# Pre-norm attention and three-matrix FFN on 8 cores: reordered head with one power per tile, 34 identity matmuls ahead of it, and a new count of folds per head pair

## The reference

```python
def _L0_attn_ref(x, Wq, Wk, Wv, Wp):          # x: (8, 2048, 1024)
    q = (x @ Wq).reshape(B, N, H, K)          # 16 heads of 64
    k = (x @ Wk).reshape(B, N, H, K)
    v = (x @ Wv).reshape(B, N, H, V)
    scores = jnp.einsum('bnhk,bmhk->bhnm', q, k) * scale
    attn = jax.nn.softmax(scores, axis=-1)
    out = jnp.einsum('bhnm,bmhv->bnhv', attn, v).reshape(B, N, D)
    return x + out @ Wp
...
def _L0_ffn_ref(x, weight, aux_weight1, aux_weight2, bias):
    h = x @ weight; h = h @ aux_weight1; h = h @ aux_weight2
    return jnp.tanh(h + bias)
...
x = x + _L0_attn_ref(_layernorm(x), Wq, Wk, Wv, Wp)
x = x + _L0_ffn_ref(_layernorm(x), weight, aux_weight1, aux_weight2, bias)
```

## Time and profile before

| | |
|---|---|
| median of 3 runs | 729.91 us (729.4 to 729.97) |
| the profiled execution's own time | 729.96 us |
| its span, slowest core (core 6) | 728.2 us |
| spans of the 8 cores | 725.1 to 728.2 us |
| mean granted clock of each core | 0.998 to 1.000 |
| PE busy / ACT busy / DVE busy / POOL busy | 681.6 / 599.4 / 264.4 / 125.3 us |
| head, to the first exponential (core 6) | 61.5 us |
| main loop, 8 head pairs | 61.5 to 622.6 us |
| tail | the rest, 105.6 us |

### The profile page before, as it was taken

The page is one execution under the profiler, slowest core; times in us unless marked ns, Lnnn a source line. Parts: engine busy times, 40 slices in busy tenths (PEclk is TensorE's granted clock), DMA queues, the critical chain, the costliest instruction groups (busy, mean ns, idle before and its releaser), DMA issues.

```text
span 728.2 us, 21958 instructions; the slowest of 8 cores (725.1 to 728.2 us)
## 1 busy us (share of the span) xinstructions
PE 681.6 (94%) x9112; PEld 432.3 (59%) x9112; DVE 264.4 (36%) x590; ACT 599.4 (82%) x600; POOL 125.3 (17%) x169
## 2 busy tenths in 40 slices
PE   1699999999999999999999999999999989999996
PEld 0465676667666765676667656665676555444443
DVE  4724322332223322322332233224322343556663
ACT  2566999999999999999999989999999899444443
POOL 5871000000000002000000000012010121366654
PEclk9999999999999999999999999999999999999999
DMA  8959700111010004610110000032024000334332
GB/s 229 283 72 166 135 9 3 16 16 16 4 16 2 2 3 69 107 17 2 17 22 12 16 2 3 2 88 88 2 41 80 1 3 2 109 124 155 134 116 116
DMA packets 13344, 41.87 MB, mean 57 GB/s; under 512 B 1600, under 2 KB 1728, under 8 KB 13248
## 3 DMA queue, kind: packets, MB, share of 16 engines
q0 software_dynamic: 5904, 15.21, 13.7%
q1 hardware_dynamic: 7056, 25.17, 10.4%
q10 hardware_dynamic: 288, 0.10, 0.1%
HBM read 46.76 MB, written 8.39 MB: 76 GB/s over the span
## 4 chain that ended last, share of the span: by engine, by line
PE 86%; DVE 4%; issue 3%; DMA 3%; ACT 3%; POOL 0%; DVEq 0%; SPq 0%; ACTq 0%; POOLq 0%
PE sc L370 18%; PE pv L398 16%; PE fl L217 14%; PE fl L256 8%; PE sc L521 5%; PE fl L343 4%; PE fl L326 4%; PE sc L464 4%; PE fl L464 3%; ACT P L382 2%; DMA aoT<-x 2%; PE fl L422 2%; PE sc L217 1%; DMA wv<-wqkv 1%; PE pv L521 1%
## 5 line engine op out<-in xcount | busy, mean ns | idle before, releaser
L382 ACT ACTIVATE P<-sc,cb 128x1024 bf16<-128x1024 f32 x512 | 528.3, 1114 | 36.4 <-PE sc L370 24.4
L398 PEld LDWEIGHTS pv<-v,P 128*128 128x128 bf16 x4096 | 157.7, 97 | 44.1 <-issue 17.2
L398 PE MATMUL pv<-v,P 128*128 128x65 bf16 x4096 | 173.5, 193 | 5.4 <-DVE ao L414 2.6
L370 PE MATMUL sc<-qT,kT 64*128 64x256 bf16 x2048 | 157.5, 272 | 1.8 <-ACT P L382 1.8
L370 PEld LDWEIGHTS sc<-qT,kT 64*128 64x128 bf16 x2048 | 78.5, 94 | 42.8 <-issue 25.2
L532 ACT ACTIVATE S<-S 128x512 f32<-128x512 f32 x32 | 20.1, 629 | 58.2 <-DVE S L528 58.2
L256 PE MATMUL fl<-wv,S 128*128 128x128 bf16 x960 | 63.6, 219 | 1.8 <-DVE aoT L429 0.4
L256 PEld LDWEIGHTS fl<-wv,S 128*128 128x128 bf16 x960 | 54.1, 98 | 12.4 <-issue 12.2
L217 PE MATMUL fl<-S,wq 128*128 128x512 bf16 x224 | 57.8, 380 | 0.5
L217 PE MATMUL fl<-S,wk 128*128 128x512 bf16 x208 | 53.5, 380 | 3.1 <-DVE ao L414 1.3
L268 DVE CAST v<-fl 128x512 bf16<-128x512 f32 x29 | 20.0, 691 | 78.8 <-PE fl L256 78.8
(11 more groups left out here) (128 smaller groups left out, 555.8 us busy)
## 6 DMA issues: line engine op xcount, KB each, us to landing
xs<-x SPq DMA_DIRECT2D x22, 512.0 KB, 6.0
out<-S SPq DMA_DIRECT2D x15, 512.0 KB, 2.9
aoT<-x SPq DMA_DIRECT2D x8, 512.0 KB, 12.7
wk<-wqkv POOLq DMA_DIRECT2D x8, 256.0 KB, 9.0
wq<-wqkv POOLq DMA_DIRECT2D x8, 256.0 KB, 4.9
wv<-wqkv POOLq DMA_DIRECT2D x8, 256.0 KB, 5.9
bufA<-w1t POOLq DMA_DIRECT2D x4, 512.0 KB, 14.3
bufB<-w POOLq DMA_DIRECT2D x4, 512.0 KB, 25.0
```

What stands on the lines that cost most here:

```text
L370: ins = TE.matmul(sc[s][:, 512 * h + QC * i:512 * h + QC * (i + 1)], kT[p % 2][64 * h:64 * (h + 1), 128 * m:128 * (m + 1)], qT[p % 2][64 * ...
L382: exp_in[t] = s_se.inc(SE.activation(P[t % NPB][:], sc[s][:], AF.Exp, bias=cb[p % 2][:], scale=0.125))
L398: ins = TE.matmul(bank[PV0][:, col:col + 65], P[t % NPB][:, off:off + 128], v[p % 2][:, VW * (2 * m + h):VW * (2 * m + h) + 65], start=(u ...
```

## The change

There are three parts.

1. **The head.** `ln1_tile` takes each tile on its own: DVE also writes minus the mean (`ngm`); POOL makes one power for the tile, and only for every fourth tile the product `nm`; the other tiles are normalised as (x + ngm) * rs, tile 15 on DVE. The first slice, `wk` of pair 0, is issued once tile 0 has landed and no longer at the start; `wk` of pair 1 is issued in group 0 of the loop. K and Q of a group now stand ahead of the transposes of the next tiles on PE, V ahead of the two after them, and K of pair 1 for the same group at the end, for groups 0, 1 and 2. The squares of groups 0 to 2 move ahead of the last K and Q. V of group 3 is cut into 12, 8 and 12 matmuls around the guards. `nm` for all tiles is made by one more DVE instruction behind the squares.
2. **34 matmuls** of the identity with itself on PE, ahead of the first transpose, once `identb` and `identf` have landed.
3. **The folds.** Pair 0 has one K unit of pair 1 less to run, since three are in the head; `N_FOLD` becomes 8, 4, 4, 4, 4, 4, 4 where it was 7, 4, 4, 4, 4, 5, 4. The lines that treat pair 3 by themselves stay.

```diff
-        w_in = {(1, 0): load_slice(1, 0)}
+        w_in = {}
...
+        def ln1_tile(t):
             need(VE, x_in[t])
...
+            m = s_ve.inc(VE.bn_aggr(mv[:, 2 * t:2 * t + 2], st[:]))
             need(VE, m)
-            m = s_ve.inc(VE.tensor_scalar(ve[:, t:t + n], var, EPS, None, ALU.add))
+            s_ve.inc(VE.tensor_scalar(ngm[:, t:t + 1], mv[:, 2 * t:2 * t + 1], -1.0, None, ALU.mult))
+            m = s_ve.inc(VE.tensor_scalar(ve[:, t:t + 1], mv[:, 2 * t + 1:2 * t + 2], EPS, None, ALU.add))
             need(GP, m, gp_ones)
+            m = s_gp.inc(GP.tensor_tensor(rs[:, t:t + 1], ve[:, t:t + 1], mhalf[:, 0:1], ALU.pow))
+            if t % 4 == 0:
+                need(GP, m)
+                nm_in[t] = s_gp.inc(GP.tensor_tensor(nm[:, t:t + 1], ngm[:, t:t + 1], rs[:, t:t + 1], ALU.mult))
+                return
+            eng, sem = (VE, s_ve) if t == NT - 1 else (GP, s_gp)
+            need(eng, m, t1_mm.get(t - 2 * NXN))
+            xn_in[t] = sem.inc(eng.tensor_scalar(xn1[t % (2 * NXN)][:], x_tile[t], ngm[:, t:t + 1],
+                                                 rs[:, t:t + 1], ALU.add, ALU.mult))
...
+        need(TE, const_in)
+        for _ in range(34):
+            TE.matmul(bank[7][:, 0:128], identb[:], identb[:], start=True, stop=True)
+        need(GP, x_in[0])
+        w_in[(1, 0)] = load_slice(1, 0)
+        for t in range(4):
+            ln1_tile(t)
+            if t == 0:
+                ln1_se(0)
+            if t == 1:
                 w_in[(0, 0)] = load_slice(0, 0)
+            ln1_turn(t, SE, s_se)
+        w_in[(2, 0)] = load_slice(2, 0)
+        for g in range(NT // 4 - 1):
+            t0 = 4 * g + 4
+            for t in range(t0, t0 + 2):
+                ln1_tile(t)
+            ln1_se(t0)
+            if g == 0:
                 w_in[(1, 1)] = load_slice(1, 1)
+            bk = first_proj(1, 0, g)
+            bq = first_proj(0, 0, g)
+            evict_qk(1, 0, g, bk, SE, s_se)
+            for t in range(t0, t0 + 2):
+                ln1_turn(t, SE, s_se)
+                if t == t0:
+                    evict_qk(0, 0, g, bq, SE, s_se)
+            for t in range(t0 + 2, t0 + 4):
+                ln1_tile(t)
+            bv = first_proj(2, 0, g)
+            if t0 + 4 == NT:
+                for h in range(3):
+                    square(1, 0, h)
+                    square(0, 0, h)
+            ln1_turn(t0 + 2, SE, s_se)
+            evict_v(0, g, bv, SE, s_se)
+            ln1_turn(t0 + 3, *((VE, s_ve) if t0 + 4 == NT else (SE, s_se)))
+            bk = first_proj(1, 1, g)
+            evict_qk(1, 1, g, bk, SE, s_se)
...
-        N_FOLD = [7, 4, 4, 4, 4, 5, 4]
+        N_FOLD = [8, 4, 4, 4, 4, 4, 4]
...
-            for g in range(2 if p == 0 else 0, 4):
+            for g in range(3 if p == 0 else 0, 4):
                 units.append(unit_k(p + 1, g))
```

More of the change, by code:

```diff
@@ L657, in build_program @@
         ring["i"] = 0
[L658 removed]
+        b = next_bank()
+        values = v_mms(0, 3, b)
+        for _ in range(12):
+            next(values)
         guard1(0, next_bank())()
```

72 lines of the change are left out of this document (10 added, 62 removed).

## The result

| | before, same chip | after |
|---|---|---|
| median | 729.94 us (729.4 to 730.28, 4 runs) | 738.71 us (737.96 to 740.56, 4 runs) |
| ratio after / before | | 1.0125, 95% interval 1.0105 to 1.0144 |
| profiled execution, slowest core | 729.96 us, core 6, span 728.2 | 740.56 us, core 4, span 738.9 |
| mean span of the 8 cores | 726.8 us | 735.1 us |

What follows compares the result with a forecast made beforehand. The prediction took PE to bound the kernel, with ACT waiting for it in the loop. From 729.96 us, -2.5 (head) - 2.7 (pair 5) + 12.0 (stall) + 1.7 (clock) - 1.3 (excess) = +7.2 gave 737.2 us, range 733.0 to 740.5.

Steps and rivals of the forecast that it cites:

- part 1, pair 5: Pair 5 of the main loop: 16 fillers instead of 17 make it 2.7 us shorter, bounds -1.7 and -3.2.
- part 2, pair 3 in all: Pair 3: the wait for w3 (+12.0), a clock restart (+1.7) and the pair's own excess dropping out (-1.3).
- part 3, head: Start to first exponential: reordered tiles, slices and PE work bring it 2.5 us sooner, bounds 0 and -4.5.
- part 4, 34 matmuls: Head, ahead of the first transpose: identity matmuls fit in idle PE time, cost 0 and gain 0.
- pair 0: First pair of the loop: one K unit less and one fold more, 16 units as before, change 0.
- tail: After the last pair: said not to be touched, so no term in the sum.
- The stall: Pair 3's first unit_w123: PE waits for late pieces of w3 and loses 12.0 us, bounds +8.4 and +13.
- The restart of the clock: Behind the wait in pair 3: one spell of PE at the lower clock, +1.7 us, bounds 0 and 3.4.
- Pair 3's own excess: Pair 3's extra 1.4 us, seen only with the w3 transfer, mostly vanishes while PE stands still: -1.3.
- (a): Pair 3: shorter stall of +8.4 as on core 0, clock stays up, 731.9 us; chance 0.18.
- (b): Head: gains nothing, as slices back to back hold K of pair 1 until 35; 739.7 us, chance 0.13.
- (c): Pair 3: the wait for w3 costs nothing and both gains remain, 724.8 us; chance 0.05.

Runs made afterwards that it cites:

- e3_folds_only: The kernel before, head untouched, with N_FOLD 7, 5, 4, 4, 4, 4, 4, so pair 1 has the 17th unit; 740.9 us, ratio 1.0158.
- e6_wk1_early: e1_plain_order with the wk slice of pair 1 issued right behind wv, ahead of tiles 4 and 5; 724.86 us, ratio 0.9935.
- e1_plain_order: The changed kernel without the two lines that pull pair 3's first fold ahead of the K units; 725.84 us, ratio 0.9959.
- e2_fold_two_units_later: The changed kernel with pair 3's first fold placed behind two K units; 729.37 us, ratio 1.0001.
- e7_head_only: The changed kernel with the old fold numbers 7, 4, 4, 4, 4, 5, 4; 729.56 us, ratio 1.0007.

## Why the prediction was right

It gave 737.2 us, 733.0 to 740.5; 738.7 was measured, and the mechanism was the one named. That the sum came within 1.5 us owes something to luck: two terms that were put at nothing cost 1.7, and pair 3 cost 0.8 less than forecast. (The ends of the range lie 0.5 and 0.8 us outside the sums that their reasons give, 733.5 for a stall of 10 without restart and 739.7 for no gain in the head.) Step by step:

| step | predicted | measured, mean of 8 cores |
|---|---|---|
| part 1, pair 5 | -2.7 | -2.6 |
| part 2, pair 3 in all (12.0 + 1.7 - 1.3) | +12.4 | +11.6; +12.2 on core 6 |
| part 3, head | -2.5 | -2.6; -1.8 over several kernels |
| part 4, 34 matmuls | 0 | 0 in the head |
| pair 0 | 0 | +0.8 |
| tail | 0 | +0.9 |
| pairs 1, 2, 4, 6, 7 | 0 | +0.2 |
| sum | +7.2 | +8.4; medians +8.8 |

**Pair 5** was right: 71.88 to 69.32, and `e3_folds_only` shows the same 2.4 to 2.7 for a 17th unit in another pair.

**The stall** was right in its place, its cause and its form: on core 4 four waits ended by `bufA`, pieces of 1.5 to 3.1 us (9.8 in sum where 11 to 12 were expected; slow matmuls between them fill the rest), and landings of the fourth piece 12.8 to 17.1 us after its issue, against the 14.0 to 17.6 of the earlier trace rows. The step that carried it was to count the landings from the first issue and to set them against the place of the reader. On core 4 the last two matmuls would have stood at 277.5 (8.8 us behind the row at 268.69, as in the earlier trace rows from 269.88 to 278.7) and stood at 289.04: 11.5 against the 12.0 forecast. The fit of the Trainium skill, *DMA: Bandwidth & Descriptors*, section "Anatomy of one DMA", would have had all four pieces there 6.8 us after the first issue; on core 4 it took 1.6 + 17.1 = 18.7, and no core was under 1.6 + 12.8 = 14.4. That estimate counts the bf16 bytes; w3 is float32 in memory, and with those 4.2 MB the same fit gives an estimate of 11.6, still less than any core took. The measurement decides against the page for four such converting loads queued together.

**The restart of the clock** was right in kind and too small: 1.7 forecast, 2.2 measured. It was taken from 8 matmuls of K in the head that ran slow. Here all of PE's work from 289.04 to 294.89 ran slow: two fold matmuls, P times V, Q times K, five of K and P times V again. The slow matmuls before that cost nothing, since the next piece was still under way. As for the 1.00 that the windows of the head read beside a slow K: the trace's clock record begins only at 27.36 there (core 6), where that K ends (23.64 + 3.57 = 27.21), and 1.00 is what the window shows where there is no record.

**Pair 3's own excess**, -1.3, was a misreading. It was read from the slowest core alone (70.58); on seven cores pair 3 was 69.2 to 69.6 before. One core's difference between two of its pairs was taken for an effect of the transfer. For core 6 itself it fits (82.77 - 70.58 = 12.2, against 12.4), for the others not. This error and the small restart both made the forecast of pair 3 too small. What made up for them is the stall itself: by the landings (landing of the fourth piece less 7.3 us) it is 7.1 to 11.3 us by core, mean 9.6, against the 12.0 forecast. As a mean 9.6 + 2.2 - 0.1 gives the 11.6 within 0.1; on core 6, 11.3 + 2.2 - 1.3 is its 12.2.

**The head** came out right as a sum in this execution, with 1.8 rather than 2.6 over several kernels, and two of its steps were off. The statistics of tile 3 began 2.2 us sooner (means of 12.19 and 14.42; 2.5 on core 6), not 1.2, so K of group 0 began at 19.75 on core 6, the core that the forecast was worked out on, not 20.3, and V at 26.21, not 27.1. V waited for `wv` on four cores only. But as worked out, K of pair 1 then waits for its slice: 31.10 against 31.2. That wait swallowed the surplus, and on cores 4 and 5 the clock fell around it, which was not foreseen; `e6_wk1_early` frees another 1.2 us by issuing the slice sooner.

**Not foreseen** were the tail and pair 0. "The tail isn't touched" holds for its instructions and not for its time. In pair 0 some cores show pauses of PE such as this, on core 1, which the trace puts down to nothing:

```profile
81.32 0.54 PE L399 MATMUL pv<-v,P 128*128 128x65 bf16 x10 [1.65 <-issue]
```

They end near 80 us, when w1 and w2 have landed (the last piece at 75.6 on this core) and the slices queued behind them come in. `e1_plain_order` has the same fillers in pair 0 and half the excess, `e2_fold_two_units_later` none, so it isn't settled. These two terms, with 0.2 in other pairs and less 0.8 in pair 3, are the 1.2 us between forecast and sum. The rivals fall: (a) a stall short enough for 731.9 occurs on single cores only (core 2, fourth piece after 12.8), and others then set the time; which cores those are isn't fixed, but goes with the order of issue in a pair of neighbours, shown below; (b) the first exponential came sooner, by 1.8 to 2.6, though `e7_head_only` shows this gain eaten elsewhere; (c) would have needed the last piece within 7.3 us.
